# Loading edge records from ScalarE's queue, four groups per chunk, instead of from SyncE's queue among the stream loads

## The chip, the cores and the metric

The kernel runs on one core of one Trainium2 chip. The metric is the device time of one execution in microseconds (us), from the first to the last instruction of the core; lower is better. Times before: 10585.76 us median of 3 runs (10540.46 to 10622.88).

## What is computed

Four graph layers follow each other on 6,250 nodes (features of 128) and 200,000 edges, each with a residual and a layer norm:

```python
edge_index = jnp.stack([src, dst])
x = _layernorm(x + L0(x, ..., src, dst, edge_type_40))     # attention: softmax over the edges of a node
x = _layernorm(x + L1(x, edge_index, W_l, W_r))            # mean over the edges, two products
x = _layernorm(x + L2(x, edge_index, edge_weight, ...))    # three weighted graph convolutions
x = _layernorm(x + L3(x, edge_index, edge_attr_64, ...))   # edge filters, summed at the SOURCE node
```

L1 is `segment_sum(x[src]) / deg @ W_l.T + x @ W_r.T`. L2 is three times `segment_sum(x[src] * w) @ W_rel.T + b + x @ W_root.T`. L3 computes a filter for every edge from its 64 attributes and sums `h[dst] * filter` by the edge's source.

## The kernel before

The kernel runs in stages, each a block in which the five engines have a program each; a stage ends when all are done. The stages up to 5275 us make edge scores and attention sums and build two dense matrices in memory, `c_dense` (how often node u is a source of node v) and `w_dense` (the same, weighted), padded to 49 blocks of 128 nodes. The last stages (after some 7840 us) do L3 over the edges, which must by then lie in memory in the order of their source node (`sorted_recs`).

The change touches the **dense stage** between the two, lines 1325 to 1613. It does L1 and the three convolutions of L2 as four passes (`PASSES`) of a dense product: the node features, 49 blocks of 128, times the matrix. One pass goes through 13 chunks of columns (`NCH`): twelve of 512 columns and a last one of 128, called the quarter chunk here. A chunk is seven stream loads (`NS`, 1792 KB each, 448 KB for the quarter chunk) with seven blocks each, so 364 loads in all. They go through a ring of four slots (`STREAMS`).

- **SyncE (SP)**, lines 1327 to 1343: for each load l it waits until the load four before it has been used (`s_used`, counted up by TensorE), issues the load (line 1339), and then issues the record loads that fall on this l (line 1332): 196 groups (`NG`) spread evenly over 364 loads, so one group after each second load, sometimes after two in a row. A record load brings 1,024 edges' records (264 KB) into one of five slots (`REC_SLOTS`) of `rec_in`. From the sixth group on it is preceded by a wait (line 1331) on `s_rput` of its slot, until the group five before it has been scattered.
- **GpSimd (POOL)**, lines 1602 to 1613: for each group it waits for the record load (`s_rin`), then issues eight indirect DMAs (line 1608) that scatter 128 records each to their place in `sorted_recs`. This is by-work for L3; nothing in the dense stage reads it.
- **TensorE (PE)**, `chunk`, lines 1406 to 1436: for each of the seven loads of a chunk, 7 blocks of matmuls (line 1423), then `s_used`. In between, after the second load (s == 1) comes `linear` of the previous chunk, after the fourth (first pass) `turn_nodes`, after the fifth (s == 4, the first three passes) `turn_results`. A matmul in float32 appears in the trace as two instructions, so a chunk has 98 on line 1423. Four chunks are the body of a loop that runs three times; the quarter chunk stands behind it.
- **ScalarE (ACT)**, lines 1467 to 1504: iteration i of 53 waits for the end of chunk i-1 and copies its sums (line 1482, `agg_t`), waits for `linear` or for VectorE's part and applies its activation, and in the first three passes ends with the copy of the turned results (line 1504), which TensorE has ready after s == 4 of chunk i. In the last pass it ends with line 1500.
- **VectorE (DVE)** normalises in the first and last pass (lines 1571 to 1598).

Of the kernel before, what the change touches and what calls it, by code (L numbers as in the profile page):

```python
# [14 lines left out]
TILES = 8  # L15
GE = TILES * P
NG = -(-N_EDGES // GE)
# [43 lines left out]
REC_SLOTS, L3_SLOTS = 5, 7  # L61
# [12 lines left out]
def build_program(nc, T, out):  # L74
    ctx = ExitStack()
    with ctx:
        def sb(name, shape, dt=f32, of=ctx):
            return of.enter_context(nc.sbuf_tensor(name, shape, dt))
# [3 lines left out]
        def sem(name):  # L82
            live.append(nc.alloc_semaphore(name=name))
            return live[-1]
# [118 lines left out]
        with nc.Block() as block:  # L203
            @block.sync
            def _(e):
                e.dma_start(consts[:, :], T["consts"][:, 0:C_SPREAD]).then_inc(s_small, 16)

                e.dma_start(spread_f[:, :], T["consts"][0:PARTS * TILES, C_SPREAD:C_WIDTH]
                            ).then_inc(s_small, 16)
                e.dma_start(src_i[:, :], T["src_c"]).then_inc(s_edge, 16)  # L210
                e.dma_start(gd[:, :], T["dst_row"][0:P, :]).then_inc(s_gd, 16)
                e.dma_start(gd2[0:NG - P, :], T["dst_row"][P:NG, :]).then_inc(s_gd, 16)
                e.dma_start(X[:, :].rearrange("p (b f) -> p b f", f=F),
                            T["x"].rearrange("(b p) f -> p b f", p=P)).then_inc(s_edge, 16)

                e.wait_ge(s_rng, 1)
                e.dma_start(range_dst[0:P, :], small[:, 4:6].bitcast(i32)).then_inc(s_rng_out, 16)
                e.dma_start(range_dst[P:NG, :], small[0:NG - P, 6:8].bitcast(i32)).then_inc(s_rng_out, 16)
                e.wait_ge(s_rng_out, 32)
                e.dma_start(table_dst[:, :], range_dst.rearrange("(a g) c -> a (g c)", a=1)).then_inc(s_rng_in, 16)  # L220
                e.wait_ge(s_rng_in, 16)
# [50 lines left out]
        def node_products(tag, parts, w_out, finish, store=None):  # L272
# [5 lines left out]
            def run(block):  # L278
                @block.tensor
                def _(e):  # L280
                    def transposes(b):
                        if b >= 2:
                            e.wait_ge(s_tc, b - 1)
                        for n, (get, _) in enumerate(parts):
                            ins = e.transpose(wide[:, 512 * (b % 2) + n * P:512 * (b % 2) + (n + 1) * P], get(b), ident)
                        ins.then_inc(s_t, 1)

                    transposes(0)
                    for b in range(NB):
                        if b + 1 < NB:  # L290
                            transposes(b + 1)
                        e.wait_ge(s_tc, b + 1)
                        if b >= 2:
                            e.wait_ge(s_f, b - 1)
                        for n, (_, w) in enumerate(parts):
                            ins = e.matmul(bank[2 + b % 2][:, 0:w_out], lhsT=tT[:, b % 2, n * P:(n + 1) * P],
                                           rhs=w[:, 0:w_out], start=(n == 0), stop=(n == k - 1))
                        ins.then_inc(s_o, 1)
# [141 lines left out]
        records = T["records"].rearrange("g p (t w) -> g p t w", w=RW)  # L440
# [864 lines left out]
        LOADS = PASSES * NCH * NS  # L1305
# [6 lines left out]
        def chunk_blocks(c):  # L1312
            return range(c * (CH // P), min((c + 1) * (CH // P), NB))

        def cols(c):
            return slice(c * CH, min((c + 1) * CH, NP_))

        rec_in = sb("dn_rec_in", [P, REC_SLOTS, TILES, RW], of=dense)
        s_rin, s_rput = ([sem(f"dn_{n}{k}") for k in range(REC_SLOTS)] for n in ("rin", "rput"))
# [5 lines left out]
        with nc.Block() as block:  # L1325
            @block.sync
            def _(e):
                def records_in(g):
                    k = g % REC_SLOTS
                    if g >= REC_SLOTS:  # L1330
                        e.wait_ge(s_rput[k], 16 * TILES * (g // REC_SLOTS))
                    e.dma_start(rec_in[:, k, :, :], records[g, :, :, :]).then_inc(s_rin[k], 16)

                for l in range(LOADS):
                    p, c, s = l // (NCH * NS), l // NS % NCH, l % NS
                    n = len(chunk_blocks(c)) * P // HB
                    if l >= STREAMS:
                        e.wait_ge(s_used, l - STREAMS + 1)
                    e.dma_start(stream[:, l % STREAMS, 0:n, :, :],
                                (c_dense if p == 0 else w_dense)[c, s, :, 0:n, :].rearrange("p h (q n) -> p h q n", n=HB)  # L1340
                                ).then_inc(s_in[l % STREAMS], 16)
                    for g in range(-(-l * NG // LOADS), -(-(l + 1) * NG // LOADS)):
                        records_in(g)

            @block.tensor
            def _(e):
# [119 lines left out]

            @block.scalar
            def _(e):
                for i in range(PASSES * NCH + 1):
                    p, c = divmod(i, NCH)  # L1470
                    if i == 0:
                        for s in range(NS):
                            e.wait_ge(s_spread, s + 1)
                            e.activation(rstd[:, s * KQ:(s + 1) * KQ], rstd[:, s * KQ:(s + 1) * KQ], ACT.Sqrt
                                         ).then_inc(s_root, 1)
                    if i:
                        pp, cc = divmod(i - 1, NCH)
                        w = len(chunk_blocks(cc)) * P
                        e.wait_ge(s_used, NS * i)
                        if i >= 3:  # L1480
                            e.wait_ge(s_lin, i - 2)
                        e.copy(agg_t[:, (i - 1) % 2, 0:w], agg_bank[(i - 1) % 2][:, 0:w]).then_inc(s_agg, 1)
                        if 0 < pp < PASSES - 1:
                            e.wait_ge(s_lin, i)
                            e.activation(nodes_t[:, cols(cc)], lin_bank[:, 0:w], ACT.Relu, bias=conv_bias[:, pp - 1:pp])
                            e.activation(turning[:, (i - 1) % 2, 0:w], lin_bank[:, 0:w], ACT.Relu,
                                         bias=conv_bias[:, pp - 1:pp]).then_inc(s_hid, 1)
                        else:
                            n = cc + 1 if pp == 0 else NCH + cc + 1
                            e.wait_ge(s_var, n)  # L1490
                            e.activation(dvar[:, 0:w // P], dvar[:, 0:w // P], ACT.Sqrt).then_inc(s_sd, 1)
                    if i < NCH:
                        e.wait_ge(s_xt, c + 1)
                        if c >= 2:
                            e.wait_ge(s_lin, c - 1)
                        e.copy(own_t[:, c % 2, 0:len(chunk_blocks(c)) * P], turn_x[:, 0:len(chunk_blocks(c)) * P]
                               ).then_inc(s_own, 1)
                    elif p == PASSES - 1:
                        e.wait_ge(s_lin, i - 1)
                        e.copy(own_t[:, c % 2, 0:len(chunk_blocks(c)) * P], nodes_t[:, cols(c)]).then_inc(s_own, 1)  # L1500
                    if 0 < i <= 3 * NCH:
                        to = nodes_t if pp == 0 else (H, X)[pp - 1]
                        e.wait_ge(s_rt, i)
                        e.copy(to[:, cols(cc)], turn_r[:, 0:w]).then_inc(s_back, 1)
# [375 lines left out]
```

## Time and profile before

| | us |
|---|---|
| median of 3 runs | 10585.76 |
| lowest and highest | 10540.46, 10622.88 |
| the profiled execution | 10540.46 (its span 10538.9) |
| dense stage in it, first to last `agg_t` copy | 5350.9 to 7828.4 |

The profiled execution is the lowest of the three, 45 us below the median. Busy times are per engine; "PEclk" is the clock granted to TensorE as a share of full speed. A view of windows gives for each stretch its length and then, for each engine, the busy time and the number of instructions in brackets. A timeline has start, duration, engine, line and operation, and in square brackets the idle time before it with what the profile takes for its releaser; where a releaser has long been done (the gather `z_got` had ended before the dense stage), it was another.

### The profile page before, as it was taken

To read this page: it belongs to the slowest core of one execution; us is meant where nothing else is said; L and a number is where in the kernel's file an instruction comes from. 1 tells how busy PE (TensorE), PEld (TensorE's weight loads), DVE (VectorE), ACT (ScalarE), POOL (GpSimd) and SP (SyncE) were. 2 spreads that over 40 slices of the span, in tenths; PEclk is the share of its full clock that TensorE was granted. 3 is DMA by queue.
4 is the path that set the end of the run, shared out by engine and by line. 5 is a ranking of instruction groups with operands and counts; after the bars stand their busy time and mean duration, and the time that the engine had idled before them with its cause. 6 is when DMAs were issued, how large, how long until landed. Compare 5 with 4: busy or idle time off the path is not lost. (4 is left out here: it accounts for less than half of the span.)

```text
span 10538.9 us, 155042 instructions
## 1 busy us (share of the span) xinstructions
PE 8012.7 (76%) x38400; PEld 4943.1 (47%) x38401; DVE 4173.5 (40%) x9924; ACT 3268.6 (31%) x5403; POOL 5543.1 (53%) x5296
## 2 busy tenths in 40 slices
PE   2988888888875666665589898998976777777766
PEld 1544444444444555555534443444444555555544
DVE  5877777743334666666521000000012222222223
ACT  3012345654555666555500000000002222222222
POOL 5888887877740000000055555656655666566654
PEclk7999999999997666666699998999987877777877
DMA  3233445665654333322277676877752222222221
GB/s 114 74 116 130 157 172 198 218 221 204 213 200 143 129 116 108 100 97 89 79 291 300 258 304 260 316 305 278 307 212 58 61 60 60 59 61 63 62 58 54
DMA packets 563154, 1661.17 MB, mean 158 GB/s; under 512 B 115313, under 2 KB 312029, under 8 KB 519494
## 3 DMA queue, kind: packets, MB, share of 16 engines
q1 hardware_dynamic: 352666, 1182.75, 30.4%
q0 software_dynamic: 206976, 473.99, 15.0%
q10 hardware_dynamic: 3312, 1.94, 0.1%
q8 instruction: 104, 1.70, 0.1%
q14 instruction: 96, 0.79, 0.0%
HBM read 1174.46 MB, written 483.82 MB: 157 GB/s over the span
## 5 line engine op out<-in xcount | busy, mean ns | idle before, releaser
L920 PE MATMUL wide<-ring 128*128 128x392 bf16 x14112 | 2525.2, 341 | 541.8 <-DVE ring L850 265.9
L527 POOL DMA_INDIRECT z_got<-z_table,z_idx x1568 | 2105.4, 1343 | 595.9 <-issue 466.8
L920 PEld LDWEIGHTS wide<-ring 128*128 128x128 bf16 x14112 | 1413.8, 100 | 1653.0 <-issue 900.2
L1699 POOL DMA_INDIRECT l_rows<-h_table,l_recs x1568 | 1572.7, 1003 | 1065.2 <-DMA l_recs<-sorted_recs 616.6
L1608 POOL DMA_INDIRECT sorted_recs<-dn_rec_in,type_f x1568 | 1525.6, 973 | 1054.6 <-DMA dn_rec_in<-in_records 585.0
L1055 POOL DMA_DIRECT2D rows<-z_edges x196 | 103.5, 528 | 2055.7 <-PE wide L362 1847.3
L1423 PE MATMUL wide<-stream,X 128*128 128x512 f32 (+1 forms) x2548 | 1090.3, 584 | 105.5 <-issue 86.0
L373 PE MATMUL wide<-rows,onehot 128*128 128x130 f32 x3904 | 861.0, 408 | 281.6 <-DVE A L390 281.6
L373 PE MATMUL wide<-l_rows,l_onehot 128*128 128x128 f32 x3904 | 648.6, 315 | 551.9 <-issue 295.3
L373 PEld LDWEIGHTS wide<-rows,onehot 128*128 128x128 f32 x3904 | 797.0, 311 | 340.2 <-DVE A L390 340.2
L373 PEld LDWEIGHTS wide<-l_rows,l_onehot 128*128 128x128 f32 x3904 | 581.3, 226 | 598.6 <-issue 323.9
L1423 PEld LDWEIGHTS wide<-stream,X 128*128 128x128 f32 x2548 | 484.2, 197 | 681.6 <-issue 661.0
L1594 DVE TENSOR_TENSOR A<-A,wide 128x512 f32<-128x512 f32 (+1 forms) x13 | 8.5, 656 | 1806.6 <-PE wide L1386 1617.3
L839 DVE TENSOR_TENSOR ring<-ring,parts 128x1536 bf16<-128x1536 bf16 (+1 forms) x394 | 692.6, 1758 | 65.8 <-issue 65.8
L1798 DVE TENSOR_TENSOR l_rows<-l_filters,l_rows 128x1024 f32<-128x1024 f32 x196 | 240.3, 1226 | 1114.8 <-ACT l_filters L1776 851.5
L836 DVE TENSOR_TENSOR ring<-iota_h,src_r 128x512 bf16<-128x512 f16 (+1 forms) x394 | 271.7, 689 | 1017.8 <-PE wide L920 659.0
L968 ACT COPY wide<-zero_f 128x784 f32<-128x784 f32 x788 | 642.1, 815 | 66.7 <-PEq L574 16.9
L984 ACT COPY A<-wide 128x784 f32<-128x784 f32 x392 | 318.1, 811 | 963.8 <-PE wide L920 859.4
L1423 PE MATMUL wide<-stream,A 128*128 128x512 f32 (+1 forms) x1274 | 556.2, 589 | 76.9 <-issue 75.1
L850 DVE TENSOR_SCALAR ring<-iota_h,slot_at 128x784 bf16<-128x784 f16 (+1 forms) x1568 | 596.5, 443 | 0.0
L1764 ACT COPY l_attr_t<-wide 64x1024 f32<-64x1024 f32 x196 | 197.2, 1006 | 1211.6 <-DMA rel_id<-in_iota 764.6
L1423 PE MATMUL wide<-stream,H 128*128 128x512 f32 (+1 forms) x1274 | 540.4, 581 | 34.3 <-issue 34.1
(262 smaller groups left out, 8748.0 us busy)
## 6 DMA issues: line engine op xcount, KB each, us to landing
stream<-w_dense SPq DMA_DIRECT2D x252, 1792.0 KB
stream<-c_dense SPq DMA_DIRECT2D x84, 1792.0 KB
z_edges<-z_got POOLq DMA_DIRECT2D x196, 528.0 KB
rows<-z_edges POOLq DMA_DIRECT2D x196, 528.0 KB
dst_bc<-in_dst_row SPq DMA_DIRECT2D x196, 512.0 KB
c_dense<-A SPq DMA_DIRECT2D x49, 1568.0 KB
w_dense<-A SPq DMA_DIRECT2D x49, 1568.0 KB
c_dense<-H SPq DMA_DIRECT2D x49, 1568.0 KB
```

The lines of the kernel that those rows point to most:

```text
L373: ins = e.matmul(sums_bank[:, 0:width], lhsT=onehot[:, t, :], rhs=group_rows[:, t, 0:width], start=(t == 0), stop=(t == TILES - 1))
L527: e.indirect_dma_start(out=z_got[:, s, t, :], out_offset=None, in_=z_table, in_offset=bass.IndirectOffsetOnAxis(ap=z_idx[:, s, t:t + 1], a ...
L836: e.tensor_tensor(to[:, :, 0, :], iota_h[:, 0:P].unsqueeze(1).to_broadcast([P, n, P]), src_r[:, bass.ds(t, n)].unsqueeze(2).to_broadcast([ ...
L839: e.tensor_tensor(to[:, :, 1:4, :], to[:, :, 0:1, :].to_broadcast([P, n, 3, P]), parts[:, bass.ds(t, n), :].unsqueeze(3).to_broadcast([P, ...
L850: e.tensor_scalar(ring[:, at:at + spans * WC], iota_h[:, 0:spans * WC], slot_at[:, bass.ds(t + k, 1)], None, ALU.is_equal).then_inc(s_made, 1)
L920: ins = e.matmul(banks[:, bass.ds(to[v], 1), int(m > 0), 0:WC].rearrange("p a x -> p (a x)"), lhsT=slots[:, k, m * P:(m + 1) * P], rhs=slo ...
L968: e.copy(pairs[k].rearrange("p (a x) -> p a x", a=2)[:, :, 0:WC], zero_f[:, 0:1].unsqueeze(2).to_broadcast([P, 2, WC])).then_inc(s_gone, 1)
L984: e.copy(staging[k][:, :, :, WN * n:WN * (n + 1)], window(n % 4))
L1423: ins = e.matmul(agg_bank[first % 2][:, 0:w], lhsT=stationary[p][:, b, :], rhs=stream[:, l % STREAMS, 0:w // HB, k, :], start=(b == 0), st ...
L1608: e.indirect_dma_start(out=sorted_recs, out_offset=bass.IndirectOffsetOnAxis(ap=pos_i[:, g * TILES + t:g * TILES + t + 1], axis=0), in_=re ...
L1699: e.indirect_dma_start(out=rows[:, k, t, :], out_offset=None, in_=h_table, in_offset=bass.IndirectOffsetOnAxis(ap=recs[:, k, t, R_DST:R_DS ...
L1798: e.tensor_tensor(rows[:, k, :, :], filters[:, g % 2, :].rearrange("p (t f) -> p t f", f=F), rows[:, k, :, :], ALU.mult).then_inc(s_msg, 1)
```

## The change

The record loads leave SyncE's program. ScalarE issues them instead: at the head of its iteration i it issues the groups below 4 (i + 1) that have not been issued, so four groups per iteration (0 to 3 in the first, 192 to 195 in iteration 48) and none after. The waits on `s_rput` move with them; the slots, the sizes and GpSimd's program stay.

```diff
             @block.sync
             def _(e):
-                def records_in(g):
-                    k = g % REC_SLOTS
-                    if g >= REC_SLOTS:
-                        e.wait_ge(s_rput[k], 16 * TILES * (g // REC_SLOTS))
-                    e.dma_start(rec_in[:, k, :, :], records[g, :, :, :]).then_inc(s_rin[k], 16)
-
                 for l in range(LOADS):
...
-                    for g in range(-(-l * NG // LOADS), -(-(l + 1) * NG // LOADS)):
-                        records_in(g)
...
             @block.scalar
             def _(e):
+                def records_in(g):
+                    k = g % REC_SLOTS
+                    if g >= REC_SLOTS:
+                        e.wait_ge(s_rput[k], 16 * TILES * (g // REC_SLOTS))
+                    e.dma_start(rec_in[:, k, :, :], records[g, :, :, :]).then_inc(s_rin[k], 16)
+
+                brought = 0
                 for i in range(PASSES * NCH + 1):
                     p, c = divmod(i, NCH)
+                    for g in range(brought, min(NG, 4 * (i + 1))):
+                        records_in(g)
+                        brought = g + 1
                     if i == 0:
```

## Rows read from the trace of the kernel before

**Rows 1.** The page: its first line.

```profile
span 10538.9 us, 155042 instructions
```

**Rows 2.** Windows: the dense stage as a whole.

```profile
5275.00:7870.00 2595.00, 2317.96 (x5943) 1080.78 (x5943) 190.43 (x747) 117.21 (x253) 1527.12 (x1570) 0.93 0.75 287
```

**Rows 3.** Waits of SyncE's queue in the stage: total us, times, longest.

```profile
SPq L1339 <- PE wide L1423: 1009.3, 183, 26.8
SPq L1339 <- DMA z_got<-z_table,z_idx: 920.4, 79, 28.2
```

**Rows 4.** The instructions on `rec_in`: durations in ns (least, median, most).

```profile
L1608 POOL DMA_INDIRECT sorted_recs<-dn_rec_in,type_f x1568: 963/970/2167, 5283.3 to 7816.4; - x196
L1332 SPq DMA_DIRECT2D dn_rec_in<-in_records x196: 332/433/1157, 5275.4 to 7793.5; - x196
```

**Rows 5.** Windows from one `agg_t` copy to the next, one chunk each.

```profile
5275.00:5350.90 75.90, 47.34 (x103) 20.75 (x104) 51.90 (x223) 3.33 (x9) 43.71 (x40) 0.80 0.76 276
...
5734.00:5793.10 59.10, 49.32 (x123) 22.50 (x122) 5.42 (x21) 1.98 (x5) 32.56 (x34) 0.88 0.66 261
...
5894.40:5925.90 31.50, 18.44 (x119) 16.60 (x118) 5.07 (x20) 1.65 (x4) 17.99 (x19) 0.78 0.50 162
...
6541.10:6586.50 45.40, 21.20 (x109) 16.27 (x109) 0.00 (x0) 2.30 (x4) 30.92 (x32) 0.67 0.50 168
6586.50:6630.20 43.70, 43.70 (x102) 19.34 (x101) 0.00 (x0) 1.20 (x5) 29.06 (x31) 0.95 0.98 374
...
6674.50:6718.90 44.40, 44.40 (x107) 19.69 (x106) 0.00 (x0) 2.39 (x4) 23.97 (x26) 1.00 0.75 278
6718.90:6772.00 53.10, 46.75 (x107) 20.50 (x106) 0.00 (x0) 2.46 (x5) 32.34 (x34) 0.94 0.73 294
...
6823.70:6876.70 53.00, 47.33 (x107) 20.63 (x106) 0.00 (x0) 2.39 (x5) 30.93 (x33) 0.94 0.71 282
...
7172.90:7217.80 44.90, 29.49 (x119) 18.43 (x119) 0.00 (x0) 2.45 (x5) 30.05 (x31) 0.80 0.63 221
...
7501.20:7554.50 53.30, 49.91 (x126) 22.63 (x125) 4.42 (x16) 1.30 (x3) 31.31 (x32) 0.98 0.79 316
7554.50:7607.80 53.30, 48.48 (x120) 21.85 (x120) 4.33 (x16) 1.31 (x4) 31.03 (x32) 0.95 0.71 282
...
7783.30:7828.40 45.10, 20.82 (x114) 18.07 (x112) 4.09 (x16) 0.98 (x4) 26.11 (x27) 0.62 0.25 74
```

**Rows 6.** Timeline of the queue of SyncE in one slow chunk.

```profile
5746.39 0.43 SPq L1332 DMA_DIRECT2D dn_rec_in<-in_records  x1
5774.87 0.80 SPq L1339 DMA_DIRECT2D stream<-c_dense  x2
```

**Rows 7.** Timelines of GpSimd, TensorE and VectorE in the same chunk.

```profile
5729.84 0.97 POOL L1608 DMA_INDIRECT sorted_recs<-dn_rec_in,type_f  x1 [12.05 <-DMA dn_rec_in<-in_records]
...
5769.31 1.16 POOL L1608 DMA_INDIRECT sorted_recs<-dn_rec_in,type_f  x1 [0.30 <-issue]
```

```profile
5747.38 0.39 PE L1368 MATMUL wide<-w_L_gnn_W_rt,own_t 128*128 128x128 f32 x2
5747.60 12.18 PE L1423 MATMUL wide<-stream,X 128*128 128x512 f32 x28
```

```profile
5761.47 1.13 DVE L1576 SCALAR_TENSOR_TENSOR A<-wide,rdeg,X 128x128 f32<-128x128 f32 x4 [58.20 <-DMA z_edges<-z_got]
```

**Rows 8.** The last quarter chunk: one window, then TensorE's and GpSimd's timelines.

```profile
7788.80:7817.30 28.50, 7.70 (x24) 5.68 (x23) 0.00 (x0) 0.00 (x0) 21.80 (x23) 0.55 0.18 54
```

```profile
7821.85 6.50 PE L1423 MATMUL wide<-stream,X 128*128 128x128 f32 x38 [0.34 <-issue]
```

```profile
7816.36 0.97 POOL L1608 DMA_INDIRECT sorted_recs<-dn_rec_in,type_f  x1 [0.30 <-issue]
```

**Rows 9.** Windows of four unbroken groups of GpSimd, and the pause behind.

```profile
7562.80:7603.30 40.50, 37.83 (x88) 16.52 (x87) 1.82 (x8) 0.71 (x2) 31.01 (x32) 1.00 0.75 300
7603.30:7615.70 12.40, 10.21 (x30) 5.43 (x30) 3.00 (x13) 1.11 (x3) 0.01 (x1) 0.72 0.59 222
```

## The prediction

> **What bounds the kernel now.** From the page I take the span, 10538.9 us [rows 1]; the rest is read from the changed stage. The windows view [rows 2] says what it is made of: 2318 us of 2595 are TensorE's, 1527 GpSimd's, ScalarE has 117, VectorE 190, and TensorE was granted 0.93 of its full clock. So TensorE sets the stage, and the question is where its other 280 us go, and whether the moved loads have to do with it.
>
> The waits of SyncE's queue [rows 3] hold a trap. 1009 us are put down to line 1423, the matmul that frees a stream slot: that is a full ring, harmless. Another 920 us, 79 times, are put down to a gather that ended before the stage. The tempting reading is that SyncE stands in the wait for `s_rput` and is late with stream loads. The timeline refutes it [rows 6]: the record load at 5746.39 goes out, and the stop of 28 us comes behind it, before the *stream* load at 5774.87, whose wait is for TensorE's `s_used`. Yet by 5759.8 TensorE was through the 28 matmuls of two more loads [rows 7]. VectorE shows the same: the last matmul of `linear` starts at 5747.4 and ends by 5747.8, VectorE, which waits for it, starts at 5761.47 [rows 7], 14 us late. What TensorE signals arrives late.
>
> When? The timeline of GpSimd has 32 indirect DMAs, four groups, in one unbroken row from 5729.84 to 5770.5 [rows 7], and SyncE comes free at 5774.87, 4 us after its end. The last quarter chunk is the cleanest case [rows 8]: in 28.5 us from 7788.8 the trace has 24 of TensorE's matmuls of 128 columns, while GpSimd issues without a pause; GpSimd's last DMA ends at 7817.3; 4.5 us later 38 matmuls go through in 6.5 us, 0.17 us each. No record load and no stream load was issued in between. So a long unbroken row of GpSimd's indirect DMAs delays TensorE's signals more and more and in the end slows TensorE itself; a short one does not.
>
> The chunk windows give the price [rows 5]. Three chunks from 6586.5 to 6718.9 take 132.4 us, 44.1 each, with 26 to 31 indirect DMAs per chunk: nearly the mean load, but in single groups with a short pause behind most. Three from 6718.9 to 6876.7 take 157.8 and two from 7501.2 to 7607.8 take 106.6, where GpSimd does its four groups unbroken: 264.4 / 5 = 52.9 each, 8.8 more. It is not how much GpSimd does in a chunk, but whether it pauses.
>
> **The change, part by part.**
>
> *SyncE's 196 issues go.* 196 x 0.43 us = 84 us of its time [rows 4]. It waits 1930 us in the stage [rows 3]; worth nothing while it waits for TensorE.
>
> *ScalarE gets 196 issues.* Four per iteration, 4 x 0.43 = 1.7 us, at the head of the iteration: behind the copy that follows s == 4 of a chunk, so with s == 5 and 6 left, 2/7 of 44.1 = 12.6 us before the next `agg_t` copy is due, or in the last pass earlier still. Covered; without that cover 48 x 1.7 = 82 us. In iteration 0 they stand ahead of the first square roots, at the start, where VectorE needs several us anyway: nothing.
>
> *The wait for `s_rput` is now in ScalarE's row.* Queued behind it are the copies of `agg_t`, for which TensorE's `linear` waits. Group g needs group g-5 scattered: of iteration i's four, the last needs the third of iteration i-1. Issued a chunk earlier, it is done after three groups of eight at 1.27 us, 30 us, and a few for landing; a chunk lasts 44 us or more. No wait in a full chunk. Only at the quarter chunks may it bite (a rival, below).
>
> *The record loads come four at a time.* This is the part that counts. GpSimd gets four groups within some us, once per chunk, and does them unbroken: 40.5 us [rows 9]. The single-group rhythm of the 44.1 us chunks can no longer occur. Nothing in before shows ScalarE's order, so I bound the chunk's time t. From below: 40.5 us for the groups, then at least 4.5 us until the signals are through [rows 8] and some 3 for `agg_t` or turn, issue and landing: 48 us. From above: the worst four-group chunk of the first pass, 59.1 us [rows 5]. I take 52.9, since five windows with just this pattern agree within 1.6 us, and what they have behind the four groups is a pause of 12.4 us [rows 9] that TensorE's own work needs too: it was slowed and must make up its instructions.
>
> *GpSimd is through 3.75 chunks earlier*, in iteration 48 of 52. The last three full chunks run at 44.1, and the last quarter chunk, 98 matmuls at 0.17 us [rows 8], takes some 15 us, not 45.1.
>
> *The start.* The first window lasts 75.9 us with 40 unbroken indirect DMAs [rows 5]; now there are 32. I take 10 us off.
>
> **The sum.** Before: 51 windows from 5350.9 to 7828.4, 2477.5 us, of which four quarter chunks are 31.5 + 45.4 + 44.9 + 45.1 = 167 and 47 full ones 2310.6, 49.2 each. After: 44 full ones at 52.9 (2328), three at 44.1 (132), three quarter chunks at about 50 (four groups and their pause fall on each, 150), the last at 15: 2625 us. That is +147, with the start +137. In short, the difference is 44 t - 2190, zero at t = 49.8. On the profiled execution (10540.5): 10,678. It is the lowest of three; on the median of 10,586: 10,723. I predict 10,720. The bounds t = 48 and 59.1 make it -78 and +410.
>
> **The rivals.**
>
> *Nothing changes.* The loads are the same, GpSimd has the same 2000 us of work, and its groups bunched up before too: about half of the chunks are slow already. If t comes out at the present mean of 49.2, the difference is 44 x 49.2 - 2190 = -25: 10,560. For it: TensorE's pause-work may overlap the four groups better in the new phase. Against it: no window with 32 unbroken DMAs is under 51 us among those I priced with.
>
> The Trainium skill (DMA: Bandwidth & Descriptors, section Issuing engines are not separate DMA queues) stands with this rival: transfers issued by different engines share the same 16 DMA engines, so spreading the issues saves only sequencer time. By it the sum would be 0; the trace agrees that SyncE's 84 us are on no path, and the rule says nothing of how GpSimd's groups bunch.
>
> *Faster: it was the shared queue.* If the 28 us stops of SyncE come of records and streams in one program, and not of GpSimd's row, they vanish: 44 windows fall to 44.1, 44 x 44.1 - 2190 = -250: 10,336. For it: the stops and the slow chunks fall together. It decides once t is under 49.8. Against it: in the last quarter chunk the slow stretch ends with GpSimd's row [rows 8], and SyncE had nothing to issue in it; VectorE and TensorE are late too.
>
> *ScalarE is blocked.* At a quarter chunk two iterations lie close, so eight groups meet five slots; ScalarE may stand up to two groups (20 us) at each of four places: +80 on the forecast, 10,800. Against it: a quarter chunk lasted 45 us so far, enough for four groups.
>
> **How the numbers follow.** The four-group chunk of 50.5 to 56 us gets 0.68: above t = 52.2 it is over 1% slower (about what a measurement of this kernel can tell from no change), so 0.56 slower and 0.12 same. Nothing changes 0.16, same. Faster 0.12. ScalarE blocked 0.04, slower. Together: faster 0.12, same 0.28, slower 0.60. t = 56 gives +274, so 10,860 is the upper end; at the lower end 10,550 takes in the case of no change; left out are the faster rival and small tails above.
>
> **What the profile after should show.** GpSimd: almost every row of indirect DMAs is 32 long, 40.5 us, with one pause per chunk, and it ends near the last quarter of the stage's final pass, four chunks before its end. Windows between `agg_t` copies: near 53 us, clock about 0.94, up to chunk 48, then 44 at clock 1.00, and a last quarter chunk of 15. Waits of SyncE's queue put down to a wrong DMA rise above 920 us. ScalarE has no wait on `s_rput` worth naming. The prediction is wrong if four-group rows come without a slow chunk (the mechanism falls), or if the rows are shorter than 32 (ScalarE issues them apart).

## The result

The changed kernel takes 10856.61 us (median of 4 runs, 10825.0 to 10877.56), the kernel before 10596.62 us (median of 4, 10540.46 to 10622.88). The ratio is 1.0265, 95% interval 1.0229 to 1.0300: slower by 2.65%, where 1.3% was forecast. The time lies at the upper end of the range that the prediction gave (10,550 to 10,860 us), but the change is twice the forecast one.

The page of the changed kernel, first line, against [rows 1]:

```profile
span 10859.2 us, 155042 instructions
```

All of the loss, 320 us between the two spans, lies in the dense stage. Its windows from one `agg_t` copy to the next (length; then busy us and instructions of TensorE, its weight loads, VectorE, ScalarE, GpSimd; clock, DMA share, GB/s), against [rows 5]:

```profile
5422.20:5480.90 58.70, 49.08 (x123) 22.25 (x122) 5.34 (x21) 1.94 (x4) 29.92 (x31) 0.88 0.64 234
...
6021.80:6070.50 48.70, 22.73 (x120) 20.21 (x119) 4.95 (x20) 1.52 (x4) 25.23 (x26) 0.61 0.37 130
...
6281.90:6334.80 52.90, 47.54 (x108) 20.64 (x107) 0.00 (x0) 2.44 (x4) 31.04 (x32) 0.94 0.71 278
6703.30:6776.20 72.90, 35.82 (x125) 19.20 (x124) 0.00 (x0) 2.43 (x4) 53.50 (x56) 0.64 0.45 159
...
7407.00:7497.40 90.40, 42.56 (x133) 21.89 (x133) 0.00 (x0) 2.44 (x4) 62.09 (x64) 0.58 0.38 129
7497.40:7528.90 31.50, 31.50 (x78) 14.19 (x78) 0.00 (x0) 1.66 (x5) 1.63 (x2) 1.00 0.98 405
7528.90:7621.20 92.30, 56.68 (x114) 22.32 (x113) 4.09 (x16) 1.30 (x3) 60.54 (x63) 0.70 0.41 148
7897.20:7955.10 57.90, 48.69 (x120) 22.75 (x119) 4.10 (x16) 1.27 (x4) 32.16 (x34) 0.91 0.69 262
...
8111.40:8155.20 43.80, 43.80 (x116) 20.40 (x115) 4.09 (x16) 1.27 (x3) 0.00 (x0) 1.00 0.57 200
8155.20:8167.90 12.70, 12.70 (x114) 12.52 (x113) 4.09 (x16) 0.98 (x3) 0.00 (x0) 1.00 0.49 145
```

Three things are to be seen. Chunks with four groups of GpSimd take 53 us in the two middle passes, but 59.6 on average in the first pass and mostly 55 to 60 in the last. At two quarter chunks the windows are far dearer, 72.9 and 90.4 us, and once more 92.3 just behind. And as soon as GpSimd is through (the last two lines, x0) a full chunk takes 43.8 us and the quarter chunk 12.7.

The waits of SyncE's queue, against [rows 3]: those put down to a gather that ended long before rise from 920 to 1324 us, the longest from 28 to 43.

```profile
SPq L1333 <- DMA z_got<-z_table,z_idx: 1323.9, 78, 43.2
SPq L1333 <- PE wide L1415: 1044.3, 191, 30.5
```

The instructions on `rec_in`, against [rows 4]: the scatters are what they were; the loads cost ScalarE's queue 445 ns each. What has changed is how the scatters follow each other. Counting a row as ended where GpSimd is idle for more than 0.6 us, the kernel before has 85 rows, 38 of them 8 DMAs long and 22 of them 32 or more; the changed kernel has 46, 43 of them 32 long and three 64.

```profile
L1610 POOL DMA_INDIRECT sorted_recs<-dn_rec_in,type_f x1568: 964/970/2049, 5299.4 to 8029.7; - x196
L1465 ACTq DMA_DIRECT2D dn_rec_in<-in_records x196: 334/445/1376, 5290.7 to 7982.4; - x196
```

From the first to the last `agg_t` copy the changed kernel takes 8167.9 - 5366.4 = 2801.5 us, the kernel before 2477.5. This number, "the 51 windows", is used for all kernels below. It differs between chips too: for the kernel before it is 2559.2 in e14, on another chip of the same kind (see below), so a difference of less than some 80 us between two chips says little.

### The profile page after: what moved, and what is told of

The parts are those of the page before. It is cut to its first block and busy times, and to the rows that moved or that the text cites. A ratio compares the mean times of both kernels' runs of the same rounds, so it can differ in the third digit from the quotient of the medians.

```text
span 10859.2 us, 155042 instructions
## 1 busy us (share of the span) xinstructions
PE 8132.9 (75%) x38400; PEld 4994.6 (46%) x38401; DVE 4174.1 (38%) x9924; ACT 3269.5 (30%) x5403; POOL 5556.4 (51%) x5296
## 5 line engine op out<-in xcount | busy, mean ns | idle before, releaser
L1415 PE MATMUL wide<-stream,X 128*128 128x512 f32 (+1 forms) x2548 | 1148.9, 604 | 221.3 <-issue 201.9
L1415 PE MATMUL wide<-stream,H 128*128 128x512 f32 (+1 forms) x1274 | 574.6, 602 | 107.8 <-issue 101.3
L379 DVE TENSOR_TENSOR l_onehot<-l_iota,l_src_f 128x512 f32<-128x512 f32 x488 | 335.2, 687 | 592.2 <-remote 438.5
```

The costliest lines, as they stand in the source:

```text
L379: return e.tensor_tensor(onehot[:, 4 * h:4 * h + 4, :], iota[:, bass.ds(b * P, P)].unsqueeze(1).to_broadcast([P, 4, P]), ids.to_broadcast( ...
L1415: ins = e.matmul(agg_bank[first % 2][:, 0:w], lhsT=stationary[p][:, b, :], rhs=stream[:, l % STREAMS, 0:w // HB, k, :], start=(b == 0), st ...
```

## The experiments

The theories: the **row theory** (the prediction's) says that an unbroken row of GpSimd's indirect DMAs slows TensorE, whoever issues the record loads. The **ScalarE theory** says that the loads and waits in ScalarE's program make it, and so TensorE, late. All kernels of the experiments have two register operations more in the stage that builds the dense matrices, a lower bound of 1 on two counts that are waited for; e1 and e14 price them.

The experiments ran on several chips, and these are of two kinds, some on which the kernel before takes about 9,584 us (e1 to e5) and some on which it takes 10,580 to 10,720 (e6 to e16, and the runs of the result); each kernel's time is compared only with that of the kernel before on the same chip.

### On chips where the kernel before takes 9,584 us

**e1**, the kernel before with the two added operations.

> The kernel before with two register operations added in the stage that builds the dense matrices (a lower bound of 1 on two counts that it waits for); every kernel of this study has them. Row theory (a long unbroken row of GpSimd's indirect DMAs slows TensorE) and ScalarE theory (record loads issued in ScalarE's program make it late) say the same: 10,600 us within 40, the 51 windows between agg_t copies again 2,480 us within 40.

Measured: 9587.55 us against 9583.87, ratio 1.0002 (0.9993 to 1.0012). The added operations cost nothing; the time was missed by 1,000 us, for the reason above.

**e2**, four groups at once, but from SyncE:

```diff
-                    for g in range(-(-l * NG // LOADS), -(-(l + 1) * NG // LOADS)):
-                        records_in(g)
+                    if l % NS == 4 or l == 0:
+                        i = 0 if l == 0 else l // NS + 1
+                        for g in range(min(NG, 4 * i), min(NG, 4 * (i + 1))):
+                            records_in(g)
```

> Record loads stay on SyncE's queue, but four per chunk come at once, behind the stream load s == 4 of a chunk. ScalarE's program is that of the kernel before. Row theory: GpSimd's rows are 32 long as in the changed kernel, so full chunks take 52 to 60 us and the time is 10,800 to 10,880. ScalarE theory: no load is in its way, so the time is that of the kernel before, 10,560 to 10,640.

Measured: 9582.71 us, ratio 0.9998 (0.9988 to 1.0008).

**e3**, ScalarE issues, spread over its iteration (`bring(n)` issues the next n groups):

```diff
+                    full = 0 if c == NCH - 1 else 1
+                    bring(1 + full)
...
                         e.copy(agg_t[:, (i - 1) % 2, 0:w], ...).then_inc(s_agg, 1)
+                        bring(full)
...
+                    bring(full if i else 2)
                     if i < NCH:
                         e.wait_ge(s_xt, c + 1)
```

> Record loads on ScalarE's queue as in the changed kernel, but in one iteration two at the head, one behind the agg_t copy and one behind the activation or square root; the quarter chunk gets one. Row theory: rows of at most three groups (24 DMAs) with a pause, full chunks of 44 to 47 us, the 51 windows 2,200 to 2,350 us, the time 10,350 to 10,500. ScalarE theory: the same number of loads and waits in ScalarE's program, in more places, so 10,850 or more.

Measured: 9570.20 us, ratio 0.9983 (0.9973 to 0.9993). The rows were not what was expected, at most three groups: 27 of the 49 are 32 DMAs long and seven are longer. ScalarE's queue in one iteration shows why,

```profile
6017.23 0.82 ACTq L1469 DMA_DIRECT2D dn_rec_in<-in_records  x2
6029.25 0.35 ACTq L1469 DMA_DIRECT2D dn_rec_in<-in_records  x1
6042.99 0.33 ACTq L1469 DMA_DIRECT2D dn_rec_in<-in_records  x1
```

The four loads go out within 26 us, while GpSimd needs 10.2 us for each group and so 30.6 for three. The next load is always there before GpSimd is through, and four groups make one row.

**e4**, the changed kernel with one group at a quarter chunk:

```diff
-                    for g in range(brought, min(NG, 4 * (i + 1))):
+                    for g in range(brought, min(NG, brought + (1 if c == NCH - 1 else 4))):
```

> The changed kernel, but a quarter chunk brings one group, not four (12 x 4 + 1 = 49 per pass, 196 in all). Row theory with the rows of eight groups as the cause of the dear quarter chunks: no row is longer than five groups, the windows that hold the last two quarter chunks with records (72.9 and 90.4, 31.5, 92.3 us in the changed kernel) shrink by 90 to 130 us together, the last quarter chunk has one group; the time is 10,740 to 10,790. If the dear windows come of ScalarE's order at a quarter chunk alone, no gain: 10,830 to 10,880.

Measured: 9569.75 us, ratio 0.9982 (0.9973 to 0.9992).

**e5**, the changed kernel itself:

> The changed kernel itself (with the two added register operations), beside the kernel before on the same chip. In the runs of the result a four-group row of GpSimd cost TensorE 8 us and more per chunk; on the chip of the first four experiments the same rows cost nothing. If the cost belongs to the chip and the kernel before takes about 9,584 us here too, the changed kernel is within 0.3% of it and its full chunks take 44.2 us. If the kernel before takes about 10,600 us here, the row theory wants the changed kernel 2 to 3% above it, with chunks of 52 to 60 us.

Measured: 9571.11 us against 9584.80, ratio 0.9987 (0.9977 to 0.9996), no change worth naming. So on these chips none of the orders matters. Windows of e5 in the middle passes:

```profile
6070.10:6114.30 44.20, 44.20 (x107) 19.82 (x106) 0.00 (x0) 2.42 (x5) 31.36 (x33) 1.00 0.95 342
...
6841.40:6885.60 44.20, 44.20 (x109) 19.85 (x108) 0.00 (x0) 2.42 (x5) 33.73 (x35) 1.00 0.80 267
```

GpSimd has its four groups in each of them, and TensorE is not idle for a moment; the 51 windows are 2150.5 us, in e1 2150.4. Neither theory is tested where there is no slow-down; the expected times of e1 to e4, all made for the other kind of chip, are misses. What e5 does show is that the changed order has no cost of its own in ScalarE's program. ScalarE did stand 260 us in 14 waits for a free record slot, as the prediction's rival "ScalarE is blocked" has it, but TensorE ran on, and the stage is no longer for it.

### On chips where the kernel before takes 10,580 to 10,720 us

**e6**, the changed kernel without the rows: one plain store in place of eight scatters. It leaves the sorting of the records out. The counts in the waits on `s_rput` follow (one landing per group, not eight).

```diff
-                    for t in range(TILES):
-                        e.indirect_dma_start(out=sorted_recs, out_offset=..., in_=rec_in[:, k, t, :], ...)
+                    e.dma_start(sorted_recs.rearrange("(g p t) w -> g p t w", p=P, t=TILES)[g, :, :, :],
+                                rec_in[:, k, :, :]).then_inc(s_rput[k], 16)
```

> The changed kernel without GpSimd's rows: one plain store per group (264 KB, the same bytes) in place of eight indirect scatters, so the records are not sorted and the last layer sums other edges; all loads as in the changed kernel. Row theory on a chip where the kernel before takes about 10,600 us: full chunks of 44 us and no late signals, about 10,200 us. On a chip where it takes 9,584 us, rows cost nothing there, so the full chunks stay at 44.2 us and the time within 0.5% of 9,570. If the scatters' traffic had a price on such a chip, the chunks would fall below 44.2.

Measured: 10208.07 us against 10578.70, ratio 0.9646 (0.9603 to 0.9690). The expected 10,200 was met. Its windows, one full chunk each:

```profile
6000.70:6044.90 44.20, 44.20 (x107) 19.77 (x106) 0.00 (x0) 2.42 (x5) 2.17 (x4) 1.00 0.89 342
```

The same loads from the same ScalarE program, the same bytes to memory, and each chunk takes 44.2 us with the clock at 1.00; the 51 windows are 2141.0 us, and no wait of SyncE is put down to the old gather any more. The whole loss, and 336 us that the kernel before loses in the same way, hang on GpSimd's indirect DMAs. Without them the 51 windows are as short as on the other kind of chip (2150.4 us in e1).

**e8 and e9**, each 512-column matmul on stream data cut into four of 128 columns, once with the rows and once with the plain stores of e6. The cut changes the sums that e8 returns (by 2.6%), and e9 leaves the sorting out too, so both serve for their timing alone:

```diff
-                            ins = e.matmul(agg_bank[first % 2][:, 0:w], lhsT=stationary[p][:, b, :],
-                                           rhs=stream[:, l % STREAMS, 0:w // HB, k, :], ...)
+                            for n in range(w // P):
+                                ins = e.matmul(agg_bank[first % 2][:, n * P:(n + 1) * P], lhsT=stationary[p][:, b, :],
+                                               rhs=stream[:, l % STREAMS, 2 * n:2 * n + 2, k, :], ...)
```

> The changed kernel with each matmul of 512 columns on stream data cut into four of 128, same columns and same sums: four times the instructions of TensorE while GpSimd's rows last. If the cost of a row is a limit on TensorE's instructions per us beside GpSimd's indirect DMAs, and this chip only has it higher, full chunks go from 44.2 us to over 60 where GpSimd has a row. If this chip has no such limit up to some 9 matmuls per us, the chunks stay at 44 to 48 us.

> The cut matmuls of the run before together with the plain stores (no rows of GpSimd, records not sorted). Full chunks of 44 to 48 us by every theory; if they are over 60 here too, the cut alone costs that and the row has no part in it.

Measured: e8 11915.66 us, ratio 1.1253 (1.1181 to 1.1326); e9 10380.19 us, ratio 0.9803 (0.9746 to 0.9861); two runs each. Windows of e9, one chunk:

```profile
6061.10:6107.00 45.90, 45.90 (x400) 44.75 (x399) 0.00 (x0) 2.43 (x4) 2.78 (x6) 1.00 0.88 331
```

Windows of e8: one chunk; then three stretches about one row of GpSimd, which runs from 6436.2 to 6476.7:

```profile
6439.90:6519.10 79.20, 53.78 (x402) 50.65 (x401) 0.00 (x0) 2.44 (x4) 30.70 (x32) 0.78 0.53 189
6435.00:6445.00 10.00, 10.00 (x92) 10.00 (x91) 0.00 (x0) 0.59 (x1) 6.80 (x7) 1.00 0.99 340
6450.00:6475.00 25.00, 7.06 (x22) 5.16 (x21) 0.00 (x0) 0.00 (x0) 19.00 (x20) 0.50 0.09 27
6480.00:6485.00 5.00, 4.33 (x23) 4.16 (x23) 0.00 (x0) 0.00 (x0) 0.00 (x0) 0.57 0.70 235
```

Four times the matmuls without a row cost 46 us instead of 44 in most chunks (ten of the 51 windows of e9 are longer, up to 59); with a row 79 instead of 53. And the row's effect has a shape: some 90 to 100 matmuls pass at full pace, then 22 in 25 us, about one per us, with 27 GB/s moved and the granted clock at 0.50, the lower of its two levels; some 4 us behind the row TensorE is back at 23 matmuls in 5 us. It is not time in a row that counts, it is the number of TensorE's instructions in it (each of these matmuls has a weight load, so the two can't be told apart). That is the piece the prediction lacked. The expectation of e8 was made for a chip of the other kind; whether the limit only lies higher there was not tried.

**e10**, the kernel of e2 again, now where rows cost:

> The kernel of the second experiment again (SyncE issues the record loads, four per chunk at once), for a chip on which the kernel before takes about 10,600 us. Row theory: as the changed kernel, 10,800 to 10,900 us, full chunks 52 to 60 us. ScalarE theory: 10,560 to 10,640 us. On a chip where the kernel before takes 9,584 us neither is tested.

Measured: 10935.31 us against 10717.65, ratio 1.0213 (1.0163 to 1.0264). ScalarE's program is that of the kernel before and the loss is there, and with it the rows of the changed kernel (45 of 32 DMAs and two of 64). The time is above the expected 10,900, but this chip's kernel before is at 10,717 and not 10,600; the ratio is as expected. A chunk of the first pass and one of the second,

```profile
5808.80:5866.90 58.10, 50.00 (x124) 23.27 (x122) 5.29 (x21) 1.98 (x5) 31.02 (x32) 0.88 0.65 258
6477.10:6530.20 53.10, 46.52 (x106) 20.48 (x106) 0.00 (x0) 2.46 (x5) 30.73 (x32) 0.92 0.73 282
```

The interval overlaps that of the changed kernel (1.0229 to 1.0300). The ScalarE theory falls; it is the bunching by four.

**e11**, the kernel of e4 again:

> The kernel of the fourth experiment again (changed kernel, one group at a quarter chunk), for a chip with a kernel before of about 10,600 us. Rows of eight groups as the cause of the dear quarter chunks: no row longer than five groups, the three quarter chunks with records and their neighbours give back 90 to 130 us, 10,730 to 10,780 us. If ScalarE's order at a quarter chunk is the cause: 10,830 to 10,880 us.

Measured: 10889.94 us against 10717.65, ratio 1.0175 (1.0126 to 1.0224). Windows: a quarter chunk and its successor, and the one place where a row of eight groups remained.

```profile
6765.50:6781.00 15.50, 13.43 (x106) 12.17 (x105) 0.00 (x0) 2.44 (x4) 7.75 (x8) 1.00 0.71 233
6781.00:6842.10 61.10, 49.90 (x103) 20.93 (x103) 0.00 (x0) 1.16 (x4) 31.04 (x32) 0.83 0.70 280
...
7511.40:7612.10 100.70, 60.55 (x115) 23.88 (x116) 4.09 (x16) 1.30 (x3) 62.08 (x64) 0.68 0.49 187
```

The quarter chunks shrink from 48.7, 72.9 and 90.4 us to 14.7, 15.5 and 15.5, as the row theory wants; but the chunk behind grows to 57 to 61, two chunks at the end get rows that they did not have, and at the start of the last pass two iterations of ScalarE still lie close, so that eight groups run in one row. The 51 windows are 2751.1 us, 50 below the changed kernel on its own chip, where 90 to 130 were expected. By the ratios (1.0175 against 1.0265) the gain is 0.9%, some 96 us, but the two intervals nearly touch (1.0224 and 1.0229). The rows of eight are a cause of the dear quarter chunks; how much of their cost came back is not settled.

**e12**, the kernel of e3 again:

> The kernel of the third experiment again (ScalarE issues, spread over an iteration), for a chip with a kernel before of about 10,600 us. Row theory: shorter rows, so below the changed kernel by 200 us at least, 10,350 to 10,600 us. ScalarE theory: the same loads and waits in ScalarE's program, 10,850 or more.

Measured: 10825.20 us against 10717.65, ratio 1.0109 (1.0055 to 1.0163). Below the changed kernel, but slower than the kernel before: a miss. Two windows,

```profile
5446.20:5509.30 63.10, 46.46 (x120) 22.33 (x119) 5.29 (x21) 1.93 (x5) 30.07 (x32) 0.86 0.63 236
6321.00:6375.20 54.20, 48.29 (x107) 20.96 (x108) 0.00 (x0) 2.40 (x5) 31.01 (x32) 0.91 0.70 284
```

are four-group chunks again, and 39 of GpSimd's 57 rows are 32 DMAs long. The edit did not make the short rows that it was to test: in e3, where no signal is late, the same kernel has its rows of 32 too, because its four loads go out within less time than GpSimd needs for three groups. So e12 does not speak against the row theory; it shows that loads spread over a program give GpSimd no pause unless they lie further apart than its work on them takes.

**e15**, the changed kernel with a pause after each group:

```diff
                             in_=rec_in[:, k, t, :], in_offset=None).then_inc(s_rput[k], 16)
+                    e.wait_ge(s_rput[k], 16 * TILES * (g // REC_SLOTS + 1))
```

> The changed kernel, but GpSimd waits after each group until its scatters have landed, so rows are 8 DMAs long with pauses of about 2 us, still four groups per chunk, issued by ScalarE. On a chip with a kernel before of about 10,600 us the row theory wants most of the loss gone: four groups take 4 x 12.2 = 49 us, so full chunks of 46 to 51 us and 10,450 to 10,700 us. If only the number of DMAs per chunk counts, nothing changes: 52 to 60 us per chunk, 10,850 us. On a chip with 9,584 us: the same within 0.3%.

Measured: 10953.00 us against 10716.82, ratio 1.0223 (1.0170 to 1.0277). A miss on the time, and a telling one. Waits of SyncE, of GpSimd, and of ScalarE in the stage, then one window:

```profile
SPq L1337 <- DMA z_got<-z_table,z_idx: 29.3, 7, 5.6
```

```profile
POOL sorted_recs L1614 <- DMA sorted_recs<-dn_rec_in,type_f: 854.0, 194, 7.5
```

```profile
ACT agg_t L1488 <- DMA sorted_recs<-dn_rec_in,type_f: 1649.9, 46, 49.5
```

```profile
6346.00:6403.80 57.80, 46.42 (x106) 20.48 (x106) 0.00 (x0) 2.48 (x5) 31.11 (x33) 0.91 0.75 260
```

With rows of 8 the late signals are gone, 29 us in place of 1324: this is the row theory's hit. But a pause lasts 854 / 194 = 4.4 us, not 2, so four groups take 4 x (10.2 + 4.4) = 58 us, which is the chunk of 57.8. GpSimd has become the bound, and it reaches TensorE through ScalarE, which stands 1650 us in its wait for a free slot ahead of the `agg_t` copy: the prediction's rival "ScalarE is blocked", brought about by the experiment.

**e7**, the kernel before with GpSimd bound to TensorE's progress:

```diff
                     k = g % REC_SLOTS
+                    turns, at = divmod(g, 4 * (NCH - 1) + 1)
+                    e.wait_ge(s_used, NS * (turns * NCH + at // 4) + 2 * (at % 4))
                     e.wait_ge(s_rin[k], 16 * (g // REC_SLOTS + 1))
```

(SyncE's program changes too: it issues a group behind the stream loads s = 0, 2, 4 and 6 of a chunk, one at a quarter chunk. The new places and GpSimd's wait were not tried apart.)

> The kernel before, with GpSimd waiting for TensorE's s_used before each group (a group each two stream loads, one at a quarter chunk), so that a late signal makes GpSimd pause. Row theory on a chip where the kernel before takes about 10,600 us: full chunks of 44 to 46 us, 10,300 to 10,400 us. On a chip where it takes 9,584 us: the same within 0.3%.

Measured: 10349.34 us against 10578.70, ratio 0.9775 (0.9733 to 0.9817), as expected; full chunks are mostly at 44.2 us in the middle passes, as expected, but at 47 to 49 in the first. Here a late signal of TensorE makes GpSimd pause. The signals are not all in time: SyncE still has 733 us of waits put down to the old gather, but none is over 18.5 us long (28.2 before), and of GpSimd's 92 rows one has 32 DMAs and 42 have 24. A row of 24 lasts 30.3 us and has 70 to 74 instructions of TensorE in the middle passes and some 80 in the others, no more than such a row lets pass.

**e13 and e16**, e7 and in the last edge stage a wait of GpSimd, before each group, for the gathers of the group before:

```diff
+                    if g:
+                        last, at = slot_of(g - 1)
+                        e.wait_ge(s_got[last], 16 * TILES * (at + 1))
```

> The gated kernel (10,349 us on such a chip), and in the last edge stage GpSimd waits before each group until the gathers of the group before have landed, a pause of about 2 us per group. Row theory: TensorE's signals are less late in that stage too, 2,666 us become 2,400 to 2,600; the time is 10,100 to 10,280 us. If pauses of 2 us are too short to matter, 10,350 us within 40; if GpSimd itself is the bound there, 196 pauses of 2 us make it 10,500 or more.

> The kernel of the thirteenth experiment again. On a chip with a kernel before of about 10,600 us: ratio 0.96 to 0.97 again. On a chip where it takes 9,584 us there are no late signals to avoid, and the last edge stage (2,106 us, of it 1,561 GpSimd's) has 196 pauses of 2 us in GpSimd's row: between no change and 250 us slower, 9,580 to 9,830 us.

Measured: e13 10310.25 us, ratio 0.9640 (0.9591 to 0.9690); e16, on another chip, 10312.92 us, ratio 0.9637 (0.9589 to 0.9684). The times are some 30 us above the expected 10,100 to 10,280, with the kernel before at 10,717 on these chips; e16 repeats the ratio, as expected. Windows of e13: a chunk of the dense stage and the last edge stage.

```profile
6024.70:6068.90 44.20, 44.20 (x107) 19.77 (x106) 0.00 (x0) 2.42 (x5) 30.50 (x33) 1.00 0.92 332
...
7736.00:10313.20 2577.20, 1887.37 (x10077) 1413.65 (x10076) 663.29 (x1327) 619.75 (x621) 1705.30 (x1568) 0.84 0.24 64
```

All four groups' worth of DMAs in 44.2 us: the number was never the trouble. The 51 windows are 2300.4 us; the last stage takes 2577 us against 2692 in e7 (10316.8 less 7625), which ran on another chip. On one and the same chip, from the last `agg_t` copy to the end is 2594 us in e16 and 2723 in e14. This version beats both kernels on this kind of chip. On the other kind it was not run.

**e14**, the kernel of e1 on this kind of chip:

> The kernel of the first experiment (the kernel before with the two added register operations). By every theory within 0.5% of the kernel before, on whichever kind of chip; it tells what the added operations cost in the other experiments.

Measured: 10713.36 us against 10716.82, ratio 0.9986 (0.9955 to 1.0018): the added operations cost nothing here either.

## Why the prediction fell short

**What held.** The reading of the waits: SyncE was late because TensorE's signals were, not because of a slot. e6 and e15 show it by taking the long rows away, e10 by leaving ScalarE alone. The rule of the Trainium skill (DMA: Bandwidth & Descriptors, section Issuing engines are not separate DMA queues), that the choice of issuing engine saves sequencer time at most, agrees with e10 against the changed kernel and with e5; the loss came from *when* the loads are issued, of which it does not speak. ScalarE's issues were covered, as costed, and it stood only 40 us in two waits for a free record slot. The middle passes came out at 52.7 and 52.6 us a chunk (632.8 / 12 and 630.8 / 12), where 52.9 was taken; the last two full chunks at 43.8 (44.1); the last quarter chunk at 12.7 (15).

**The step that failed** is "I take 52.9" for every chunk, and the 50 us for a quarter chunk. Of the forecast for the 51 windows, +147, measured is +324; the 177 between them divide so:

- First pass, 11 full chunks: 655.4 us, 59.6 each, not 52.9: +74. The prediction had the 59.1 us chunk in its rows and used it as an upper bound only. The traces show what makes it. First the changed kernel from the start of a row of GpSimd to the first stop of TensorE of more than 1.5 us, in a first-pass chunk, a middle one and the third quarter chunk:

```profile
5478.50:5507.10 28.60, 28.60 (x82) 13.69 (x80) 2.96 (x13) 0.59 (x1) 21.89 (x23) 1.00 0.78 312
6285.40:6323.30 37.90, 36.48 (x87) 15.77 (x85) 0.00 (x0) 1.27 (x2) 29.06 (x30) 1.00 0.79 312
7407.50:7419.50 12.00, 11.23 (x86) 9.88 (x84) 0.00 (x0) 1.39 (x3) 9.24 (x10) 1.00 0.71 247
```

  28.6, 37.9 and 12.0 us, but 82, 87 and 86 instructions: a row lets some 80 to 90 of them through, as e8 had it, whatever time they take. Then e5, where nothing holds TensorE up, in one row of the first pass and one of a middle pass:

```profile
5425.90:5466.40 40.50, 40.50 (x114) 19.40 (x113) 5.30 (x21) 1.96 (x4) 31.04 (x32) 1.00 0.96 330
6068.80:6109.20 40.40, 40.40 (x98) 18.11 (x97) 0.00 (x0) 2.43 (x4) 30.92 (x32) 1.00 0.94 334
```

  A first-pass row of 40.5 us would hold 114 instructions and a middle one 98; in the changed kernel the whole row has 87 in the one and 88 in the other. So 27 are left over in the first pass and 10 in the middle passes; at the pace of e5 that is 9.6 and 4.1 us (an estimate), a difference of 5.5 where the chunks' losses against e5's 44.7 and 44.2 us differ by 6.4. The clock adds to both: after the stop it is granted at 0.50 and a 512-column matmul takes 1.01 us instead of 0.59, for 17 us in that first-pass chunk and 7 in the middle one (which fits the 0.88 and 0.94 of the windows under the result). What the clock costs by itself was not tried.
- Last pass, up to the window that ends at 8009.9: 512.5 us for nine, not 476: +36. The three windows about the third row of eight groups (31.5, 92.3 and 45.6 us) are 11 above three of 52.9, and the six behind them, 54.8 to 59.5 us, are 25 above. The three chunks behind: +13, since the first of them still has a row's end.
- The three quarter chunks with groups: 48.7 + 72.9 + 90.4 = 212, not 150: +62. The prediction held that a quarter chunk is long enough for four groups and that a pause follows. That is so at the first (48.7); at the others ScalarE's next four loads come before GpSimd is through. ScalarE's timeline of the changed kernel at the third,

```profile
7402.91 2.00 ACTq L1465 DMA_DIRECT2D dn_rec_in<-in_records  x4
...
7440.02 1.78 ACTq L1465 DMA_DIRECT2D dn_rec_in<-in_records  x4
7497.45 0.27 ACT L1484 COPY agg_t<-wide 128x128 f32<-128x128 f32 x1 [56.85 <-DMA z_got<-z_table,z_idx]
```

  37 us between two lots of four groups that take 40.5: GpSimd has an unbroken row of 64, from 7407.5 to 7488.8, in which most of a quarter chunk's 98 short matmuls fall. The prediction named this place, but as a wait of ScalarE worth 80 us at a chance of 0.04; it was a row twice as long, and e11 takes it back in part.
- The middle passes: -6. The last quarter chunk: -2.

The 10 us that the forecast took off the start did not come: from the first stream load to the first copy are 75.7 us (5290.7 to 5366.4), before 75.9. The stages ahead took 16 us longer and what follows the last copy 19 us less, some 4 us together, in stages that the change does not touch.

So the mechanism was right as far as it went, and its size was not: t was read from windows in which the row fell on 512-column matmuls almost alone (88 instructions in 40.5 us in [rows 9]), and applied to chunks whose rows would hold 114, and a bound that sat in the rows was given too little weight. The prediction had no term for the number of TensorE's instructions in a row. That the middle passes came out at 52.7 and 52.6 us is no luck: they have just the pattern that was priced.

## What to carry to other kernels

When a wait is put down to something that ended long ago, look at what else should have released it and how late that is; here it was TensorE's own signals, held back while another engine issued indirect DMAs without a pause. Side work on GpSimd beside a dense TensorE stage wants short lots with pauses, tied to the progress of the engine that it must not disturb (e7, e13), and not loads merely spread over some places of another engine's program, if these lie closer together than the lots take (e3 and e12). Run such a change on more than one chip: the same two kernels differ by 2.65% on one kind and by 0.13% the other way on another.

## What was not expected of the hardware

- The two kinds of chip: 9,584 us against 10,580 to 10,720 for one and the same kernel. Between the traces of the kernel before and e1, 945 us apart, 327 of them lie in the 51 windows and 564 behind the last `agg_t` copy, where the last edge stage gathers. On the first kind a row of GpSimd may be hundreds of DMAs long (two of 256 and one of 384 in e5) and no full chunk takes over 44.7 us. What distinguishes the chips is open.
- Indirect DMAs beside a busy TensorE are not enough for the loss. In the first 2700 us of the kernel before, GpSimd is busy for 2067 us, mostly with gathers, and TensorE for 2125 us with 11,872 matmuls; in e1, on the other kind of chip, these are 2065 and 2151 us with 12,049. There a small copy and 0.8 us of idle time follow every eight gathers. Whether that is what spares this stage was not tried, and how short a pause suffices is open.
- On the second kind a row of 32 indirect DMAs in the dense stage lets some 80 to 100 of TensorE's matmuls pass, then about one per us (e8: 22 in 25 us), and TensorE is back about 4 us after its end. What holds them up is open. That every time here comes from an execution that was recorded, and that the traces of the second kind hold about half of the first kind's records of semaphore updates (64,907 for the kernel before, 123,849 for e1), would fit a path that signals and records share, but that is argued and not shown; whether an execution that nobody records has the slow-down was not tried.
- With the stream loads running, the scatters of a group take 4.4 us to land after the last is issued (e15), twice what was assumed.
